# Edge MLP's first layer in a graph network kernel: from a true fp32 product to one fp32r product over 96 rows of split inputs

## The reference

```python
x = layernorm(x + lstm_part(x, edges))          # LSTM over 17 gathered rows per node, then a linear layer
x = layernorm(x + message_part(x, edges))

# message_part
s, v = x[:, :32] @ W_up_s / sqrt(32), einsum(x[:, 32:], W_up_v) / sqrt(32)
h = silu(edge_attr_8 @ A1 + b1)                 # [E, 8] x [8, 64]: the layer that the change touches
h = silu(h @ A2 + b2)                           # [E, 64] x [64, 64]
w0, w1, w2, w3 = split(h @ A3, 4)               # [E, 64] x [64, 128]
ss, vs = s[src], v[src]
messages = products of ss, vs, edge_attr_4 and w0..w3     # [E, 256]
message = segment_sum(messages, dst) / 10
out = message @ W_out (scalars and vectors apart)
```

## Time and profile before

| what | value |
|---|---|
| median of 3 runs | 2734.8 us (2728.58 to 2737.38) |
| the profiled execution's own time | 2727.58 us |
| its span in the trace | 2725.8 us |
| edge stage in the trace | 1365 to 2669 us |
| PE busy | 2131.8 us (78%), 10250 instructions |
| DVE busy | 1571.8 us (58%), 3518 instructions |
| ACT busy | 1519.3 us (56%), 4753 instructions |
| POOL busy | 1585.9 us (58%), 1672 instructions |
| mean granted TensorE clock | 0.881 |

### The profile page before, as it was taken

How to read it: one execution, slowest core, us unless ns; L and a number is a source line. 1 busy time by engine, 2 the same in 40 slices (tenths; PEclk the granted TensorE clock), 3 DMA queues, 4 the chain that set the end, 5 groups by cost and what they waited for, 6 DMA issues and landing times. The chain is left out here.

```text
span 2725.8 us, 32746 instructions
## 1 busy us (share of the span) xinstructions
PE 2131.8 (78%) x10250; PEld 1643.8 (60%) x10250; DVE 1571.8 (58%) x3518; ACT 1519.3 (56%) x4753; POOL 1585.9 (58%) x1672
## 2 busy tenths in 40 slices
PE   6488888888888888888768767777777777777776
PEld 4467767777776777767645545554554555555555
DVE  5356666666666665666735555554554555555557
ACT  3455454545455555454556656656666666666662
POOL 1666666666666666666166665665665665665660
PEclk8689999999999999898977888888887888888889
DMA  8666666666666666666111111111111111111111
GB/s 304 203 185 201 204 197 175 169 177 174 182 175 179 179 177 169 176 174 181 47 52 46 47 44 44 48 43 45 47 43 43 48 44 46 50 48 40 45 43 48
DMA packets 121049, 309.60 MB, mean 114 GB/s; under 512 B 29058, under 2 KB 42604, under 8 KB 120876
## 3 DMA queue, kind: packets, MB, share of 16 engines
q0 software_dynamic: 93264, 273.00, 36.0%
q1 hardware_dynamic: 27612, 34.51, 3.8%
HBM read 288.14 MB, written 19.26 MB: 113 GB/s over the span
## 5 line engine op out<-in xcount | busy, mean ns | idle before, releaser
L664 POOL DMA_INDIRECT sender<-table,src_index x832 | 785.8, 945 | 539.3 <-issue 286.9
L369 POOL DMA_INDIRECT shared<-gates,seq_index x833 | 789.1, 947 | 502.4 <-issue 221.2
L759 ACT ACTIVATE bank<-bank,attr 128x64 f32<-128x64 f32 x3328 | 702.3, 362 | 3.9 <-issue 3.6
L392 PE MATMUL bank<-ident,shared 128*128 128x128 f32 x3332 | 497.9, 294 | 230.7 <-DVE h_lo L467 155.2
L445 ACT ACTIVATE bank<-bank,bias 128x512 f32<-128x512 f32 (+1 forms) x663 | 401.1, 634 | 494.7 <-PE bank L404 322.9
L392 PEld LDWEIGHTS bank<-ident,shared 128*128 128x128 f32 x3332 | 425.1, 152 | 321.5 <-DVE h_lo L467 187.0
L713 PE MATMUL bank<-msg,select 128*128 128x256 f32 x1664 | 504.0, 455 | 2.1 <-DVE msg L806 2.1
L795 DVE TENSOR_TENSOR side<-sender,bank 128x192 f32<-128x192 f32 x416 | 147.0, 353 | 598.4 <-ACT bank L759 394.1
L698 PEld LDWEIGHTS bank<-a,h 64*128 64x128 f32 x1664 | 238.2, 218 | 378.9 <-issue 255.2
L698 PE MATMUL bank<-a,h 64*128 64x128 f32 x1664 | 281.1, 318 | 196.4 <-ACT bank L759 138.0
L713 PEld LDWEIGHTS bank<-msg,select 128*128 128x128 f32 x1664 | 356.8, 225 | 85.8 <-issue 9.3
(11 more groups left out here) (88 smaller groups left out, 2161.9 us busy)
## 6 DMA issues: line engine op xcount, KB each, us to landing
shared<-gates,seq_index POOLq DMA_INDIRECT x833
sender<-table,src_index POOLq DMA_INDIRECT x832
gates<-shared SPq DMA_DIRECT2D x49, 256.0 KB, 4.0
feats<-attr_in SPq DMA_DIRECT2D x13, 256.0 KB
x<-x_nodes_in SPq DMA_DIRECT2D x12, 256.0 KB
table<-up SPq DMA_DIRECT2D x12, 256.0 KB, 2.3
out<-x SPq DMA_DIRECT2D x12, 256.0 KB
shared<-x_t_in SPq DMA_DIRECT2D x3, 704.0 KB, 10.2
```

What stands on the lines that cost most here:

```text
L369: pool.indirect_dma_start(out=rows[:, k % SLOTS, j, :], out_offset=None, in_=t["gates"], in_offset=bass.IndirectOffsetOnAxis(ap=seq_index[ ...
L392: last = pe.matmul(bank[:, j * P:(j + 1) * P], rows[:, k % SLOTS, j, cols], ident[:], is_transpose=True, start=(j == 0), stop=False, skip_ ...
L664: pool.indirect_dma_start(out=sender[:, hg % 4, j, :], out_offset=None, in_=t["table"], in_offset=bass.IndirectOffsetOnAxis(ap=src_index[: ...
L759: last = act_e.activation(wy[:, j, :, k, :], w[:, 2 * i + j, :, min(k, 1), :], ACT.Copy, scale=attr[:, k, tile:tile + 1])
```

## The change

The 8 inputs of each edge are brought in three times. Of two groups at a time (a pair), 32 rows of inputs stand on partitions 0 to 31, again on 32 to 63 and again on 64 to 95. ScalarE copies all 96 rows x 512 columns to fp32r (`high8`); VectorE overwrites rows 32 to 63 with input minus high part (`low8`). The weights are split in the same way, with the low part of the weights in rows 64 to 95. One fp32r product over 96 rows then sums high x high, low x high and high x low. `high8(n)` stands at the head of every second loop turn of ScalarE, `low8(n)` behind every fourth `messages` of VectorE; both are two pairs ahead at the start. `feats` has one buffer of 96 rows x 2048 columns (768 KB a load, 13 loads), and the next load waits for the last `low8` on it. Some buffers (`feats`, `wrap`, `sums_t`) move into free space behind the sums.

```diff
+SPLIT = 96
+PAIRS = GROUP // 2
-        a1 = sb("a1", [P, GROUP * P])
+        a1 = sb("a1", [SPLIT, 2 * P])
-        feats = sb("feats", [P, 2, 512])
+        spare = shared[:, NODE_TILES * MSG:NODE_TILES * MSG + PAIRS * 512]
+        feats = spare[0:SPLIT]
+        parts8 = sb("parts8", [SPLIT, 2, PAIRS, 512], F32R)
+        a1_parts = sb("a1_parts", [SPLIT, 2 * P], F32R)
...
                     for s in range(EDGE_TILES // SUPER):
-                        if s >= 2:
-                            sp.wait_ge(e_p1, GROUP * (s - 1))
-                        sp.dma_start(feats[:, s % 2, :], t["attr8"][s]).then_inc(e_feats[s % 2], 16)
+                        if s:
+                            sp.wait_ge(e_low, PAIRS * s)
+                        sp.dma_start(feats, t["attr8"][s]).then_inc(e_feats, 16)
...
                         s, b = divmod(g, SUPER // GROUP)
-                        if b == 0:
-                            pe.wait_ge(e_feats[s % 2], 16 * (s // 2 + 1))
+                        pair, which = divmod(b, 2)
+                        if g == 0:
+                            pe.wait_ge(e_a1, 2)
+                        if which == 0:
+                            pe.wait_ge(e_low, PAIRS * s + pair + 1)
                         if g:
                             pe.wait_ge(e_h2, g)
-                        pe.matmul(mlp_bank[:], a1[:, b * P:(b + 1) * P], feats[:, s % 2, :],
+                        pe.matmul(mlp_bank[:], a1_parts[:, which * P:(which + 1) * P], parts8[:, s % 2, pair],
                                   start=True, stop=True).then_inc(e_p1, 1)
...
+                    def high8(n):
+                        if n >= PAIRS * NSUPER:
+                            return
+                        s, pair = divmod(n, PAIRS)
+                        if pair == 0:
+                            act_e.wait_ge(e_feats, 16 * (s + 1))
+                        if s >= 2:
+                            act_e.wait_ge(e_p1, GROUP * (s - 2) + 2 * pair + 2)
+                        act_e.activation(parts8[:, s % 2, pair], feats[:, pair * 512:(pair + 1) * 512],
+                                         ACT.Copy).then_inc(e_high, 1)
...
+                    act_e.activation(a1_parts[:], a1[:], ACT.Copy).then_inc(e_a1, 1)
+                    high8(0)
+                    high8(1)
                     for g in range(2):
                         silu1(g)
                         silu2(g)
                     for g in range(NGROUP):
+                        if g % 2 == 0:
+                            high8(g // 2 + 2)
                         by_attributes(4 * g)
...
+                    low = slice(32, 64)
+
+                    def low8(n):
+                        if n >= PAIRS * NSUPER:
+                            return
+                        s, pair = divmod(n, PAIRS)
+                        here = parts8[low, s % 2, pair]
+                        dve.wait_ge(e_high, n + 1)
+                        dve.tensor_tensor(here, feats[low, pair * 512:(pair + 1) * 512], here.bitcast(F32),
+                                          ALU.subtract).then_inc(e_low, 1)
+
+                    dve.wait_ge(e_a1, 1)
+                    dve.tensor_tensor(a1_parts[64:SPLIT], a1[64:SPLIT], a1_parts[64:SPLIT].bitcast(F32),
+                                      ALU.subtract).then_inc(e_a1, 1)
+                    low8(0)
+                    low8(1)
...
                         messages(hg)
+                        if hg % 4 == 0:
+                            low8(hg // 4 + 2)
                         selections(hg + 1)
...
-    a1 = np.zeros((P, GROUP, 2, 64), np.float32)
+    a1 = np.zeros((3, 2, 2, 8, 2, 2, 64), np.float32)
...
-    for b in range(GROUP):
+    for which in range(2):
         for r in range(2):
-            a1[16 * b + 8 * r:16 * b + 8 * r + 8, b, r] = i["L1_gnn_A1"]
+            a1[:, which, r, :, which, r] = i["L1_gnn_A1"]
```

More of the change, by code:

```diff
@@ L40 @@
 NGROUP = EDGE_TILES // GROUP
+NSUPER = EDGE_TILES // SUPER
 NHALF = 2 * NGROUP
@@ L632, in build @@
         select = sb("select", [P, RING, HALF, P])
-        wrap = sb("wrap", [P, EDGE_TILES])
+        wrap = spare[:, EDGE_TILES:2 * EDGE_TILES]
         e_rel, e_turn = sem("e_rel"), sem("e_turn")
-        e_feats = [sem("e_feats0"), sem("e_feats1")]
+        e_feats, e_high, e_low, e_a1 = (sem(n) for n in ("e_feats", "e_high", "e_low", "e_a1"))
         e_gather = [sem(f"e_gather{i}") for i in range(4)]
@@ L640, in build @@
         e_side, e_free, e_next = (sem(n) for n in ("e_side", "e_free", "e_next"))
-        e_sems = [e_rel, e_turn, *e_feats, *e_gather, e_p1, e_h1, e_p2, e_h2, e_w, e_scaled,
+        e_sems = [e_rel, e_turn, e_feats, e_high, e_low, e_a1, *e_gather, e_p1, e_h1, e_p2, e_h2, e_w, e_scaled,
                   e_sel, e_msg, e_half, e_acc, e_side, e_free, e_next]
@@ L847, in _ @@
                     with pool.If(rounds > 1):
-                        step = feats[:].rearrange("p s n -> p (s n)")[:, 0:EDGE_TILES]
+                        step = spare[:, 0:EDGE_TILES]
                         pool.tensor_scalar(dst[:], dst[:], -float(P), None, ALU.add).then_inc(e_next, 1)
@@ L872, in _ @@
                             pool.sem_clear(s)
-        sums_t = sb("sums_t", [P, 2, 2, CHUNK])
+        sums_t = spare.rearrange("p (a b n) -> p a b n", a=2, b=2)
         f_po, f_sum, f_mom, f_sqrt, f_rstd, f_norm, f_st, f_out, f_w, f_turn, f_low, f_high = (sem(n) for n in (
@@ L976, in lay_out @@
     a["attr8"] = (np.pad(i["edge_attr_8"], ((0, epad), (0, 0)))
-                  .reshape(EDGE_TILES // SUPER, SUPER // GROUP, 2, HALF, P, 8)
-                  .transpose(0, 1, 2, 5, 3, 4).reshape(EDGE_TILES // SUPER, P, HALF * P))
+                  .reshape(NSUPER, PAIRS, 2, 2, HALF, P, 8)
+                  .transpose(0, 2, 3, 6, 1, 4, 5).reshape(NSUPER, 1, SPLIT // 3, PAIRS * HALF * P))
+    a["attr8"] = np.broadcast_to(a["attr8"], (NSUPER, 3, SPLIT // 3, PAIRS * HALF * P))
+    a["attr8"] = a["attr8"].reshape(NSUPER, SPLIT, PAIRS * HALF * P)
     a["w_ih"] = i["L0_gnn_w_ih"].T
@@ L990, in lay_out @@
     a["w_up"] = up
-    a1 = np.zeros((P, GROUP, 2, 64), np.float32)
+    a1 = np.zeros((3, 2, 2, 8, 2, 2, 64), np.float32)
     a2 = np.zeros((P, P), np.float32)
-    for b in range(GROUP):
+    for which in range(2):
         for r in range(2):
-            a1[16 * b + 8 * r:16 * b + 8 * r + 8, b, r] = i["L1_gnn_A1"]
+            a1[:, which, r, :, which, r] = i["L1_gnn_A1"]
     for r in range(2):
         a2[64 * r:64 * r + 64, 64 * r:64 * r + 64] = i["L1_gnn_A2"]
-    a["a1"] = a1.reshape(P, GROUP * P)
+    a["a1"] = a1.reshape(SPLIT, 2 * P)
     a["a2"] = a2
```

## The result

The changed kernel takes 2759.1 us, the kernel before 2734.4 us on the same chip (medians of 15 runs each): ratio 1.0088 [1.0056, 1.012], slower by 0.9% or 24 us. The forecast was 2690 us, 45 us faster. One run of the kernel before took 9031.5 us; the ratio compares the fast runs alone. The profiled execution has a span of 2757.3 us against 2725.8.

The account below looks back on a forecast made before the run. The edge stage was taken as bound by two interlaced rings of waits between ScalarE and TensorE, no engine being full. Terms -64 + 14 + 2 + 3 = -45 us took 2734.8 to 2690 us, range 2630 to 2765.

Parts of the forecast that it names:

- the first term: TensorE, edge stage: mlp1 as one fp32r product saves up to 86 us; three quarters taken, -64 us.
- rival 2: TensorE, edge stage: less work lowers the granted clock; deciding below 0.78, at 0.75 +45 us, 2780; chance 0.07.
- ScalarE's +14: ScalarE, edge stage: 52 high-part copies of 0.53 us, 28 us, half of it hidden by waits: +14 us.
- VectorE's +2: VectorE, edge stage: 52 low-part subtractions, 36 us, nearly all covered by idle time: +2 us.
- The start, +3: Edge stage start: later load, copy and subtraction delay the first product, net +3 us (ends -1 and +7).
- The new waits: Edge stage: mlp1 waiting for low8 and high8 for its load cost nothing, both being ready in time.
- Rival 1: Edge stage: the mlp2 and silu2 turns set the pace and the copies lengthen them: +35 us, 2770; chance 0.15.
- The prediction's last sign: Edge stage: if silu1's wait shrinks and silu2's grows by as much, the saving only moved.
- Rival 1's own sign: TensorE's wait for the scaled weights before mlp3 grows by 20 us or more.
- Rival 3: Edge stage: TensorE's completions are not delayed by its own work; copies and saving cancel, within 8 us, 2735; chance 0.12.
- Rival 4: Edge stage: TensorE is really short of time, so each microsecond taken off shows twice: -95 us, 2640; chance 0.16.
- GpSimd is no floor yet: GpSimd, edge stage: gathers and issue gaps sum to 1073 us, 10.3 us a group, against 12.54 us a group.

Follow-up runs that it names:

- z1: Changed kernel with splits and loads for the first two super-tiles only, later groups multiplying old inputs: 2800.4 us, 1.0008 of the kernel before.
- z2: Kernel before with a further 768 KB load to unused space beside each load of feats: 2801.6 us, 0.9994 of the kernel before.
- x3: Changed kernel with its fp32r product made four times into the same bank: 2766.5 us, 1.0084 of the kernel before.
- y1: Changed kernel with slot numbers in SBUF and three idle fp32r products of 384 columns behind each mlp product: 2826.6 us, 1.0111 of the kernel before.
- x1: Changed kernel with splits for the first two super-tiles only, short product and 768 KB loads kept: 2746.7 us, 1.0049 of the kernel before.
- x2: Kernel before, fp32 product kept, with the copy and subtraction added into a buffer nobody reads: 2757.8 us, 1.0057 of the kernel before.
- z3: Changed kernel with its 13 loads of 768 KB cut into 52 of 192 KB: 2809.2 us, 1.0025 of the kernel before.
- x7: Changed kernel without VectorE's subtractions, the second 32 rows holding the high part again: 2811.3 us, 1.0075 of the kernel before.
- x8: Changed kernel with the copy to fp32r moved from ScalarE to VectorE, ahead of the subtraction: 2799.9 us, 1.0044 of the kernel before.
- x4: Changed kernel with ScalarE's copy moved from behind silu2 to behind silu1: 2749.5 us, 1.0056 of the kernel before.
- y2: Kernel before with slot numbers in SBUF and three idle fp32 products of 128 columns behind each mlp product: 2920.5 us, 1.0441 of the kernel before.
- y5: Kernel before with slot numbers read from SBUF instead of PSUM bank 7, a control: 2796.5 us, 0.9993 of the kernel before.
- the first four groups: Four of five groups of follow-up kernels, each run on one chip with the kernel before, which took 2739.4, 2788.5, 2797.1 and 2798.7 us.
- y3: Changed kernel with its fp32r product made twelve times: 2941.5 us, 1.0513 of the kernel before.

## Why the prediction was wrong, step by step

**The step that failed** is the first term: "Saved: 0.86 - 0.23 = 0.63 us at full clock [...] I take three quarters, -64 us". Its length was right enough: the product is single and shorter, 68.0 us busy instead of 123.5, though one takes 654 ns in the mean and not the 0.4 us named. What it saved on the path was nothing: `z1` shows +0.1% within -6 and +11 us. Two things stand against the saving. Both are measured; only the second is needed, and what lies behind it is open.

- The clock. Every kernel with the single product and no added products lost 0.014 or more of the clock of the whole program, and the other products took 40 of the 55.5 us back, 44 of 63 in `z1` against `z2` on one chip (`x3` and `y1`, with more fp32r work, lost 0.009 and 0.007 of the clock). That this cost the kernel time is not shown: `x3` has TensorE busy for 80 us more and takes no longer. This is rival 2's mechanism, given 0.07. Its deciding point of 0.78 was not reached, since at 0.81, 0.80 up to 2200 us, the products together are still 15.5 us less busy (530.6 + 288.4 + 128.3 + 68.0 against 504.0 + 281.1 + 122.2 + 123.5). The Trainium skill (TensorE: Matmul & The Clock Gate, "HAM oscillation — how this bites in real kernels") says that a TensorE left waiting between bursts of matmuls is put back to the half rate, and that this is paid again each time. The trace agrees so far that the lighter product came with the lower clock, 0.81 against 0.85.
- The array time is not on the path. The single product or four of it gave the same time (`x3`). The waits of the silus, 475 and 480 us, stand there with either product. The argument "mlp1's completion is what silu1 waited for in 88 of 104 cases" took a wait for a product as a wait for its length: of silu1's 236 us only 72 lay ahead of mlp1's recorded end, so that 64 us saved would have been nearly all of them, and the change took 39 away there and gave 27 back in front of silu2. The prediction had itself noted completions 2.6 us behind the modelled end, with no row to tell why; that delay is what the silus wait for in the main (337 of 475 us), it was as long behind a long product as behind a short one (`x1`, `x2`, `x3`), and where it is absent (fast chip) the silus hardly wait.

**ScalarE's +14 and VectorE's +2** held as a sum: `x2` measured +16 us [+6, +25]. That the forecast's 16 met it so closely is in part luck: the interval is wide, and on another chip the changed kernel with its loads cut up (`z3`) stands only 5 us above the product alone (`z1`). How the cost divides is not shown; `x7` and `x8` lean to ScalarE, as the prediction had it, without resolving it.

**The start, +3**: 2.5 us. **The loads** free: 4.1 us of waiting, once; `z2` 0.9994. **The new waits** free: no row of mlp1 waits for low8 after the first, and VectorE's selections made TensorE's loads wait 3.6 us (4.5 before). **fp32r, 96 rows as 128**: not separable, and without weight.

With the failed term at 0 the prediction's own sum is 14 + 2 + 3 = +19 us; measured +24 [+15, +33]. The other terms hold to within what the runs can tell.

**Rival 1** (slower, the other ring, +35 us) came nearest in sign. The prediction's last sign, a wait moved from silu1 to silu2, is in the rows (68 us less and 73 more). Rival 1's own sign, 20 us more of TensorE waiting for the scalings, is not there by name: 138.0 and 102.4 us became 132.5 and 79.6, though the whole idle time before mlp3 grew from 196.4 to 245.9 us. And its reason is not shown: taking the copy out of that ring (`x4`) moved the time by no more than the error. **Rival 3** is borne out in what it said of the product, as far as that the delay behind mlp1's end did not change with mlp1's length, and was wrong in the rest: there was no saving for the copies to cancel. **Rival 4** fell with `x1`, `x3` and `z1`.

**"GpSimd is no floor yet"**, at 10.3 us a group, held in the first traces, where a group takes 12.7 us with the change. On the fast chip it is the floor: 1054 us for 104 groups, 10.1 each. There the price of the change, +0.7%, seems to have another source than on the slower chips, and nearly the same size.

**Open.** Why added work on TensorE counts (`y2`, 124 of 135 us) while removed work does not. The rows show where: in `y2` silu1's wait behind mlp1's recorded end is 403 us, against 210 in `y5`, so that three fp32 products behind mlp1 lengthen the delay itself; the fp32r fillers of `y1` do not (144, and 135 in the changed kernel). Not why. What delays the completions on the slower chips and not on the fast one. The changed kernel itself was not run in the first four groups, so its parts are compared with it across chips only.

## What to carry to other kernels

Before counting a shortened instruction as saved, ask whether the wait behind it is as long as the instruction or is a fixed delay behind its end: a row that starts 2.6 us after its releaser's end will do so after a shorter one too. Only the part of the wait that lies ahead of the releaser's end can be saved by shortening it. A change that thins out TensorE's work in a stage with gaps should be priced with the clock that it will then be granted, and the helper instructions that it adds to other engines have a price of their own: 16 us here for 68 us of added busy time (`x2`). Doubling or quadrupling the disputed instruction, and the new part alone without its helpers, are cheap experiments that would have told this before the change was built.

## What the runs showed of the hardware that was not expected

- Chips differ for one program: the kernel before takes 2734 to 2739, 2788 to 2799 and 2268 us. On the slower ones the silus wait some 480 us, 337 (before) and 353 (after) of them behind the recorded end of their product, on the fast one 91 (changed kernel), 3 of them behind it.
- A VectorE instruction that reads both operands from SBUF can lengthen a GpSimd gather that runs beside it: 0.95 to 1.27 us in 38 of 832 gathers, all beside a subtraction of 32 x 512, yet at most 1.11 us with the same subtractions placed behind a copy (`x8`); the selections with one operand in PSUM leave gathers at 945 ns in the mean, and they take 987 with both in SBUF (`y5`).
- The granted clock of the program was higher with added fp32r products (on one chip 0.864 with one, `x1`, and 0.870 with four, `x3`; on another 0.867 before and 0.878 with twelve, `y3`) and not with added fp32 ones (`y2`: 0.866 of 0.867).
- A lighter product slowed its neighbours: 44 us more for the three unchanged products when mlp1 was 63 us shorter, at a stage clock of 0.79 against 0.83 (`z1`, `z2`).
